# A two-layer mixer on one core: joining and finishing the first layer's results on GpSimd, two pairs of PSUM copies on ScalarE

## What is computed

```python
xn = layernorm(x)                                  # x: (2, 1024, 128)
s  = causal_attention(xn, WQ, WK, WV, 16 heads of 8) @ WO
g  = silu(moe_top2(xn, gate, w1, w2, w3))          # 8 experts, each token goes to 2, results weighted
x  = x + s * g
xn = layernorm(x)
s  = xn + recurrence_mlp(xn)                       # cumulative sums, sin/cos, layernorm, gelu
g  = silu(capacity_moe(xn, router, w0, w1, wo))    # top-2 of 8 experts with capacity 64
x  = x + s * g
```

## Time and profile before

| | us |
|---|---|
| median of 3 runs (lowest, highest) | 619.52 (618.65, 619.96) |
| the profiled execution | 619.71 |
| its span in the trace | 617.9 |
| stretch behind the first experts, to the last `pv` | 359 to 411 |

### The profile page before, as it was taken

The page is one execution under the profiler, slowest core; times in us unless marked ns, Lnnn a source line. Parts: engine busy times, 40 slices in busy tenths (PEclk is TensorE's granted clock), DMA queues, the critical chain, the costliest instruction groups (busy, mean ns, idle before and its releaser), DMA issues.

```text
span 617.9 us, 11935 instructions
## 1 busy us (share of the span) xinstructions
PE 571.0 (92%) x3875; PEld 353.1 (57%) x3902; DVE 475.7 (77%) x1307; ACT 330.8 (54%) x602; POOL 191.1 (31%) x221
## 2 busy tenths in 40 slices
PE   2878999999999999999999988988899999999996
PEld 1433544444454534999999953444446666656554
DVE  6799889999989898455555579657689899976465
ACT  2752667676777676655555468753232642262224
POOL 1450000000254452133333311000007686688400
PEclk9798899999999999999999999998899999999999
DMA  8945727060813271111111043124010322421322
GB/s 196 234 145 204 243 73 216 2 215 2 224 42 100 67 210 32 44 49 47 47 47 47 25 130 90 70 70 120 0 46 15 90 63 59 123 87 40 103 68 68
DMA packets 55611, 57.99 MB, mean 94 GB/s; under 512 B 8650, under 2 KB 39402, under 8 KB 55514
## 3 DMA queue, kind: packets, MB, share of 16 engines
q1 hardware_dynamic: 51242, 50.56, 29.2%
q0 software_dynamic: 4320, 6.81, 3.5%
HBM read 41.96 MB, written 18.85 MB: 98 GB/s over the span
## 4 chain that ended last, share of the span: by engine, by line
PE 72%; DVE 17%; ACT 4%; issue 4%; DMA 1%; SPq 1%; ACTq 0%; DVEq 0%
PE banks L1690 11%; PE banks L1832 9%; PE banks L1963 7%; PE banks L1779 6%; PE banks L1757 6%; PE banks L1702 6%; DVE banks L1240 5%; PE banks L1952 5%; PE banks L1949 5%; PE banks L2014 4%; DVE mpart L1243 3%; ACT arena L809 2%; PE banks L1651 2%; PE banks L1760 2%; PE banks L1599 1%
## 5 line engine op out<-in xcount | busy, mean ns | idle before, releaser
L809 ACT ACTIVATE arena<-banks 128x512 f32<-128x512 f32 (+1 forms) x304 | 154.3, 583 | 75.2 <-PE banks L1760 40.7
L1240 DVE CUSTOM_DVE_ANT_0 banks<-banks,arena 128x512 f32<-128x512 f32 (+3 forms) x256 | 119.8, 511 | 9.3 <-PE banks L1779 8.4
L1779 PE MATMUL banks<-arena 96*128 96x512 bf16 (+3 forms) x384 | 113.5, 336 | 7.0 <-DVE mpart L1240 3.2
L1757 PE MATMUL banks<-arena 128*128 128x512 bf16 (+3 forms) x358 | 106.5, 327 | 3.9 <-ACT arena L809 3.3
L1243 DVE TENSOR_REDUCE mpart<-banks 128x1 f32<-128x512 f32 x128 | 85.8, 684 | 9.1 <-PE banks L1779 8.0
L1690 PE MATMUL banks<-arena 128*128 128x128 f32 x624 | 76.3, 275 | 1.0 <-ACT arena L743 1.0
L1690 PEld LDWEIGHTS banks<-arena 128*128 128x128 f32 x624 | 72.8, 192 | 1.5 <-ACT arena L743 1.5
L1832 PE MATMUL banks<-arena 128*9 128x512 f32 (+3 forms) x768 | 70.7, 487 | 0.0
L852 ACT ACTIVATE arena<-banks 125x512 f32<-125x512 f32 (+2 forms) x48 | 28.4, 595 | 71.2 <-PE banks L1949 46.2
L1757 PEld LDWEIGHTS banks<-arena 128*128 128x128 bf16 x384 | 37.8, 99 | 49.5 <-issue 23.6
L620 POOL DMA_INDIRECT results<-arena x39 | 37.7, 967 | 77.4 <-DVE arena L1134 77.4
(11 more groups left out here) (295 smaller groups left out, 868.3 us busy)
## 6 DMA issues: line engine op xcount, KB each, us to landing
k_parts<-arena SPq DMA_DIRECT2D x6, 768.0 KB, 7.4
arena<-in_L_ffn_experts_w_dram SPq DMA_DIRECT2D x2, 2048.0 KB, 11.0
arena<-results SPq DMA_DIRECT2D x8, 512.0 KB, 6.8
arena<-k_parts SPq DMA_DIRECT2D x7, 576.0 KB
arena<-q_parts SPq DMA_DIRECT2D x28, 144.0 KB
arena<-in_L_ffn_w_kernel_dram SPq DMA_DIRECT2D x8, 344.0 KB, 3.6
slots<-in_pad_rows_dram SPq DMA_DIRECT2D x1, 2535.0 KB, 12.1
arena<-slots SPq DMA_DIRECT2D x39, 65.0 KB, 1.8
```

The costliest lines, as they stand in the source:

```text
L809: act.activation(Pr[:, r % 4, heads[0]:heads[-1] + 1, 0:n], ring_e[e % 3][:, 0:len(heads) * n].rearrange("p (j c) -> p j c", j=len(heads)) ...
L1240: ins = dve.tensor_tensor_reduce(unmasked, unmasked, tail_mask[:, 512 - n:512], 1.0, -BIG, ALU.add, ALU.max, part[:, at:at + 1])
L1757: ins = pe.matmul(ring_e[e % 3][:, at * n:at * n + n], QK[:, slot, j, 1, P * kt:P * kt + P], QK[:, slot, j, 0, q:q + n], start=True, stop= ...
L1779: ins = pe.matmul(ps[:, at * n:at * n + n], QK[0:TALL, slot, j, 0, P * i:P * i + P], QK[0:TALL, slot, j, 1, 512 * half:512 * half + n], st ...
```

## The change

Four things move, and nothing is computed otherwise:

- the copies of `attn_turn` and `attn_out` go from VectorE to ScalarE; the ring's table then names `aT0_sb` and `s0_sb` for these banks
- the joins of `combine` go from VectorE to GpSimd (`joined`)
- the multiplications and additions of `finish` go from VectorE to GpSimd (`added`)
- VectorE's `norm` waits for `x1_done`, which GpSimd raises

```diff
+            elif step[0] == "attn_turn":
+                frees.append(("aT0_sb", step[1] + 1))
+            elif step[0] == "attn_out":
+                frees.append(("s0_sb", step[1] + 1))
...
+            def joined(c):
+                tiles = slice(8 * c, 8 * c + 8)
+                pool.wait_ge(ld_y[c], 32)
+                pool.tensor_tensor(ya[:, tiles, :], ya[:, tiles, :], yb[:, tiles, :], ALU.add).then_inc(Z["f_done"], 1)
+
+            def added(c):
+                tiles = slice(4 * c, 4 * c + 4)
+                pool.wait_ge(Z["gated"], 1)
+                pool.wait_ge(Z["s0_sb"], c + 1)
+                pool.wait_ge(Z["ld_posr"], 16)
+                pool.tensor_tensor(ya[:, tiles, :], ya[:, tiles, :], s_sb[:, tiles, :], ALU.mult).then_inc(Z["r0_done"], 1)
+                pool.wait_ge(Z["r0_done"], c + 1)
+                pool.tensor_tensor(x1[:, tiles, :], x1[:, tiles, :], ya[:, tiles, :], ALU.add).then_inc(Z["x1_done"], 1)
...
+                    elif step[0] == "combine":
+                        joined(step[1])
+                    elif step[0] == "finish":
+                        added(step[1])
...
+                    elif step[0] == "attn_turn":
+                        c, unit = step[1], UNIT_OF[step]
+                        act.wait_ge(Z["m_ready"], unit + 1)
+                        act.copy(attnT0[:, 512 * c:512 * c + 512], ring_m[unit % 4]).then_inc(Z["aT0_sb"], 1)
+                    elif step[0] == "attn_out":
+                        c, unit = step[1], UNIT_OF[step]
+                        act.wait_ge(Z["m_ready"], unit + 1)
+                        act.copy(s_sb[:, 4 * c:4 * c + 4, :], ring_m[unit % 4].rearrange("p (n d) -> p n d", d=D)).then_inc(Z["s0_sb"], 1)
...
-                    elif step[0] == "combine":
-                        combine(ld_y[step[1]], 32, step[1])
-                    elif step[0] == "attn_turn":
-                        c = step[1]
-                        dve.tensor_copy(attnT0[:, 512 * c:512 * c + 512], unit_ready()).then_inc(Z["aT0_sb"], 1)
-                        dve.wait_ge(Z["aT0_sb"], c + 1)
-                        dve.sem_inc(Z["m_free"], 1)
+                    elif step[0] in ("attn_turn", "attn_out"):
                         unit += 1
-                    elif step[0] == "attn_out":
-                        c = step[1]
-                        dve.tensor_copy(s_sb[:, 4 * c:4 * c + 4, :], unit_ready().rearrange("p (n d) -> p n d", d=D)).then_inc(Z["m_free"], 1)
-                        unit += 1
-                    elif step[0] == "finish":
-                        if step[1] == 0:
-                            dve.wait_ge(Z["m_free"], FREES[unit - 1][1])
-                            dve.wait_ge(Z["ld_posr"], 16)
-                        link(finish(0, step[1]))
                     elif step[0] == "norm":
+                        dve.wait_ge(Z["x1_done"], 2)
                         (norm_moments, norm_rows)[step[1]](0)
```

More of the change, by code:

```diff
@@ L373, in build @@
             r_done p2_done mem_set zero_o x2_done wg_ps wg_done el_done sqrt_in sqrt_out
-            y1_done disp_ps disp_sb oh_ready dest_in sin_done u1_ps g1_ps hid1_done act1_done gate_zero tail_zero xn1_ready refined full_sb r1_done rem1_done sum_in aT0_sb xT0_sb ld_vecs ld_iota"""
+            y1_done disp_ps disp_sb oh_ready dest_in sin_done u1_ps g1_ps hid1_done act1_done gate_zero tail_zero xn1_ready refined full_sb r1_done rem1_done sum_in aT0_sb s0_sb x1_done xT0_sb ld_vecs ld_iota r0_done"""
         Z = {n: sem(n) for n in names.split()}
```

## The result

| | before | after |
|---|---|---|
| median, six runs each | 619.74 us (618.01 to 620.23) | 624.11 us (623.38 to 626.33) |
| the profiled execution, its span | 619.71, 617.9 | 623.51, 621.7 |

The ratio is 1.0077 [1.0057, 1.0097]: slower by 0.8%. The forecast was 621.8 us with a range to 623.2. Its direction was right, its size was not: it had +2.25 us, and +4.4 us came.

A forecast was written before the change was run, and what follows sets the result against it. Between 359 and 411 us the late chain ran over TensorE and ScalarE. 0.65 us gained from the copies, joins free, the norm 2.7 us later: net +2.25 on 619.52 gives 621.8 us, range 620.0 to 623.2.

The forecast's parts named there:

- The last step of the sum: Behind the routing product: the end of attention, the loads and the second layer all follow the 2.25 us delay, without slack.
- step 3 of part 3: Finish on GpSimd, queued behind `negated`: four instructions of 1.13 to 1.15 us, 4.8 us in all, ending at 388.05 us.
- The part 1 gain: Four ring copies moved to ScalarE: TensorE waits less for VectorE near 363 us, 0.65 us gained, ScalarE's cost hidden.
- The joins: Two joins on GpSimd before the gate's Silus: 2.3 us each, second ending at 376.3 us, margin 1.1 us, nothing paid.
- `negated`: On GpSimd after VectorE's last reduction: 1.22 us instead of 2.86 once the finish leaves VectorE, ending at 383.24 us.
- VectorE stood 6.4 us before the norm: VectorE waiting for GpSimd's finish: idle some 6 us, the norm starting at 388.1 us, 2.7 us later.
- TensorE's weight load: Loading the turned rows: TensorE waits for the norm's rows until 394.0 us instead of 391.57, 2.45 us late.
- The rival that the joins contend with the maxima: Before the gate: joins slowed to 6 us by VectorE's maxima, gate waits 4.6 us, 626 us in all; chance 0.05.
- any gain beyond 0.55 us: Rivals before 380 us: TensorE gains more from lighter VectorE, 619.5 to 620.7 us, chance 0.18; faster, 617.8 us, chance 0.07.
- step 6: From the turned rows to the routing product: 0.3 us given back as ScalarE catches up, 0.1 lost; net 2.25 us later.

The follow-up runs named there:

- n3: The kernel before with only the four ring copies moved from VectorE to ScalarE: 621.73 us, ratio 1.0022.
- k1: The changed kernel with the finish ahead of the last `negated` on GpSimd, TensorE's pause at the gate filled with eleven unread matmuls: 620.38 us, ratio 1.0010.
- k5: The changed kernel with the finish ahead of `negated`, unread matmuls filling the gate's pause and the old pause behind attention: 618.85 us, ratio 0.9987.
- the two repaired kernels: The changed kernel with the finish back on VectorE (622.12 us), and with the finish ahead of the last `negated` on GpSimd (621.59 us).
- the late norm: The kernel before with four unused VectorE instructions between finish and norm, making the norm 2.9 us later: 625.51 us, ratio 1.0096.
- k3: The changed kernel with unread matmuls filling TensorE's pauses at the gate and before the turned rows: 624.24 us, ratio 1.0078.
- n2: The changed kernel with only TensorE's pause before the turned rows filled, by fourteen unread matmuls: 624.11 us, ratio 1.0077.
- n1: The kernel before with the norm 2.9 us later and twelve unread matmuls in TensorE's pause before the turned rows: 625.75 us, ratio 1.0090.
- k4: The kernel before with four unread f32 matmuls filling TensorE's 1.97 us pause at 422 us, behind attention: 619.15 us, ratio 0.9979.
- q1: The kernel before with the ring copies on ScalarE, plus 0.55 us of unread matmuls putting attention's end back: 619.67 us, ratio 0.9993.
- q3: The kernel before with 1.7 us of unread matmuls added in attention: 623.05 us, ratio 1.0050.
- q4: The kernel before with 3.5 us of unread matmuls added in attention: 622.64 us, ratio 1.0062.
- q2: The kernel before with 0.55 us of unread matmuls added in attention: 620.68 us, ratio 1.0018.
- the last pair: On another chip, before with 2.8 us of unread matmuls (629.15 us, 1.0029) and the changed kernel with 0.65 us of them (629.15 us, 1.0027).

## Why the prediction was wrong

Two steps failed. The last step of the sum passed the delay on unchanged through the rest of the kernel and put the clock at nothing; there some 1.5 us were lost, which is more than the range had left. And step 3 of part 3 made the finish 0.3 us too short.

**What held.** The order of the effects was right, and each of its signs. The part 1 gain: the reduction came 0.54 us early, counted from the experts' end (21.83 us before, 21.29 after), forecast 0.65. The joins: 2.36 us each, forecast 2.3, and nobody waited. `negated`: 1.23 us, forecast 1.22, and it is slow just where VectorE's two-input instructions run beside it. VectorE stood 6.4 us before the norm, forecast some 6. TensorE's weight load came 33.91 us behind the experts' end instead of 30.98, so 2.9 us late, forecast 2.45. The rival that the joins contend with the maxima is out, and so is any gain beyond 0.55 us: the three kernels with the copies, an undisturbed finish and the full clock in the stretch (n3, k1, k5) have it at 50.14 to 50.15 us.

**The term that was mis-sized.** Step 3 of part 3 took a GpSimd instruction of 128x512 at 1.13 to 1.15 us, from the pair at 35 us; the trace has 1.15 for each of them. The four took 1.26 to 1.28 us. From the end of `negated` to that of the last they need 5.1 us (381.53 to 386.63) against 4.8, since they follow each other a little closer than was assumed. The operands are of the same shape and type (those at 35 us are subtractions, not additions as the prediction has it; the finish's multiplications and additions take the same); why they take a tenth longer was not tested. It is not VectorE's work beside them, since VectorE was idle (6.43 us in the row above), and they took the same 1.26 to 1.27 us with the finish ahead of `negated`. This gives 0.3 us, the smaller gain of part 1 another 0.1, and so does the hand-over from the rows to TensorE's weight load. In step 6, I had TensorE get back 0.3 us less 0.1 of its delay at the routing; from 2.93 us late at the weight load to 2.8 at the end of attention it got back 0.15. So the schedule is +2.8 in the trace and +3.0 in the runs at equal clock, not +2.25. That alone would have been 622.3 to 622.5 us, inside the range.

**What was missing.** The sum ended with "The end of attention, the loads behind it and the second layer all follow", as if a delay were passed on unchanged through 200 us of TensorE work. This is the step that put the forecast outside its range. The delay is not passed on unchanged where the clock differs: after's runs have a mean clock of 0.974 against 0.978 in before. The profiled execution lost 2.85 us between 412 and 451 us, where the change has no instruction; over the runs it was some 1.5 us. No rival had that mechanism. Before's own rows could have raised it: the 1.97 us pause at 422 us, the clock of 0.66 behind it, and three runs of one kernel that differ by 1.3 us.

**What stays open.** Why the changed kernel has the lower clock was narrowed, not settled. That it is lower is no chance of a few runs: before's four batches on three chips have mean clocks of 0.9775 to 0.9778, and after, the two repaired kernels, the late norm and the copies alone 0.974 to 0.975. Shown: filling the new pauses gives nothing back (k3, n2, n1), and filling the old one at 422 us raises the clock of before and of a repaired kernel (k4, k5). Not shown, only made likely by q1: that it isn't the copies as such. Supported by q1 and q3 against q4, contradicted by q2, and absent on the chip of the last pair: that the position of that pause in time decides. Mean clocks of 12 runs are uncertain by about 0.001, 0.4 us, and this is too coarse to map it further.

**A better version.** None beats before by more than a measurement can tell. The nearest are before with the pause at 422 us filled (0.9979 [0.9958, 0.9999]) and the joins alone (0.9985 [0.9964, 1.0007]).

## What to carry to other kernels

An instruction is cheap on an idle engine only if it can start when its inputs are there: here GpSimd was idle for 6.7 us, but the finish stood behind `negated`, whose input came last, and so the one consumer with a margin of 0.3 us got its rows 2.9 us late. The same move with the finish ahead cost nothing in schedule: the stretch is then as short as with the copies alone. And compare two kernels at equal mean clock as well as by their medians: a change of a microsecond or two can be schedule or clock, and only the first was also there on the chip of the last pair. But an estimate at equal clock from a dozen runs is no better than 0.3 us or so: q2 shows 1.3 us there for 0.55 us of added work.

## What was unexpected of the hardware

- A run's time followed its mean granted clock at 0.44 us per 0.001, fitted in common over 20 kernels (the five large batches of before alone give 0.37 to 0.44 each), and the mean clock of a kernel's runs moved between 0.974 and 0.982 with pauses of 2 us being filled or moved.
- One chip ran the kernel before in 626.45 us, 6.7 us longer than the three others; at a clock of 0.978 it would still be 624.6.
- Four GpSimd instructions of the same shape and type took 1.27 us each in one place and four took 1.15 in another, while VectorE was idle at the former.
